# A lead of four tiles instead of three in a graph-and-attention block, with three steps put in another order

## The reference

```python
xn = layernorm(x)
agg = segment_sum(xn[src], dst); ah = agg / max(degree, 1)
lin = xn @ W1.T + b1 + ah @ W2.T + b2
q, k, v = relu(xn @ Wq.T), relu(xn @ Wk.T), xn @ Wv.T        # 16 heads of 32
att = (q @ (k.T v)) / (q @ sum(k) + eps);  x2 = x + lin + att @ Wp.T + bp
xn2 = layernorm(x2)
pooled = sum(xn2 * softmax(xn2 @ attn_w));  gates = softmax(pooled @ gate_w + gate_b)
out = x2 + sum over the best 2 of 8 experts: g_e * gelu(gelu(xn2 @ w1_e + b1_e) @ w2_e + b2_e)
```

## Time and profile before

| | us |
|---|---|
| Runs shown (3): median | 1580.96 |
| Runs shown: lowest, highest | 1580.53, 1581.2 |
| The profiled execution | 1580.07 |
| Its span | 1578.3 |

### The profile page before, as it was taken

One profiled execution on the slowest core, in us unless ns is written; L12 is line 12 of the kernel. 1 busy time (PEld: TensorE's weight loads), 2 busy tenths in 40 slices (PEclk: granted clock), 3 DMA queues, 4 the chain that ended last, 5 costly groups with the idle time before them and its releaser, 6 DMA issues.

```text
span 1578.3 us, 29172 instructions
## 1 busy us (share of the span) xinstructions
PE 1519.8 (96%) x7597; PEld 733.7 (46%) x7598; DVE 1003.1 (64%) x2154; ACT 604.5 (38%) x997; POOL 799.0 (51%) x847
## 2 busy tenths in 40 slices
PE   5999999989999999999999999999999989999997
PEld 2444444444544444444444444444544444444443
DVE  7576522246666667666677666666666666666777
ACT  5777721111333333332333333333333335555554
POOL 4122143646777767777767777767777710000000
PEclk8999999999999999999999999999999989999998
DMA  9977776957777767777767777767777723322323
GB/s 237 262 170 190 189 179 132 217 151 208 234 235 234 234 209 231 234 234 237 233 206 239 239 240 233 234 209 236 236 233 233 233 80 120 107 90 96 106 87 112
DMA packets 166610, 308.64 MB, mean 196 GB/s; under 512 B 71986, under 2 KB 74572, under 8 KB 166260
## 3 DMA queue, kind: packets, MB, share of 16 engines
q0 software_dynamic: 62720, 205.57, 44.3%
q1 hardware_dynamic: 36112, 58.90, 11.7%
q10 hardware_dynamic: 67684, 42.96, 10.7%
HBM read 255.02 MB, written 39.49 MB: 187 GB/s over the span
## 4 chain that ended last, share of the span: by engine, by line
PE 70%; POOL 14%; issue 6%; DVE 3%; DMA 1%; ACT 0%; DVEq 0%; SPq 0%; ACTq 0%
POOL ring L522 14%; PE bank L549 13%; PE bank L554 13%; PE bank L550 12%; PE bank L622 8%; PE bank L623 8%; PE bank L708 2%; PE bank L709 2%; PE bank L710 2%; PE bank L742 2%; PE bank L747 2%; PE bank L743 2%; PE bank L793 1%; PE bank L838 1%; PE bank L800 1%
## 5 line engine op out<-in xcount | busy, mean ns | idle before, releaser
L522 POOL DMA_INDIRECT ring<-table,src_col x784 | 753.5, 961 | 328.9 <-issue 254.5
L622 PE MATMUL bank<-ring,onehot 128*128 x830 | 316.1, 381 | 14.8 <-issue 6.2
L623 PE MATMUL bank<-ring,onehot 128*128 x830 | 315.5, 380 | 0.0
L1238 DVE TENSOR_TENSOR onehot<-bank,dst_col 128x512 f32 x244 | 168.8, 692 | 96.5 <-issue 61.1
L961 ACT ACTIVATE work<-bank,rd 128x512 f32<-128x512 f32 x49 | 33.7, 687 | 336.4 <-DVE rd L1271 336.3
L549 PE MATMUL bank<-wts,xT 128*128 128x512 f16 x392 | 149.1, 380 | 4.1 <-DVE wts L1313 4.1
L550 PE MATMUL bank<-wts,xT 128*128 128x512 f16 x392 | 149.0, 380 | 0.0
L549 PE MATMUL bank<-wts,work 128*128 128x512 f16 x392 | 148.2, 378 | 0.2 <-DVE work L1441 0.2
L550 PE MATMUL bank<-wts,work 128*128 128x512 f16 x392 | 148.3, 378 | 0.0
L622 PEld LDWEIGHTS bank<-ring,onehot 128*128 x830 | 80.9, 97 | 126.5 <-issue 45.6
L623 PEld LDWEIGHTS bank<-ring,onehot 128*128 x830 | 81.1, 98 | 84.8 <-issue 0.9
(11 more groups left out here) (284 smaller groups left out, 2732.5 us busy)
## 6 DMA issues: line engine op xcount, KB each, us to landing
ring<-table,src_col POOLq DMA_INDIRECT x784, 3.7
x_rows<-work ACTq DMA_DIRECT2D x49, 256.0 KB, 3.7
work<-in_x ACTq DMA_DIRECT2D x48, 256.0 KB, 4.3
ring<-x_rows SPq DMA_DIRECT2D x12, 1024.0 KB, 5.3
out_x<-ring SPq DMA_DIRECT2D x12, 1024.0 KB
table<-xT SPq DMA_DIRECT2D x45, 256.0 KB, 3.5
ring<-in_x SPq DMA_DIRECT2D x42, 256.0 KB, 3.7
xT<-in_L_mix_qkv_weight SPq DMA_DIRECT2D x2, 1024.0 KB, 10.1
```

Source lines behind the costliest of these rows:

```text
L522: pool.indirect_dma_start(ring[:, n, :], None, table[:, :], bass.IndirectOffsetOnAxis(ap=ap, axis=0)).then_inc(slot_loaded[n], 16)
L622: mm(ps_agg[:, :], w[:, k, :], rows[:, k, 0:D], start=start, stop=False, skip_group_check=True)
L623: r = mm(ps_agg[:, :], w[:, k, :], rows[:, k, D:2 * D], start=False, stop=stop, skip_group_check=True)
L1238: V.tensor_tensor(onehot[:, bass.ds((q + t) % OG * U, U), :], ps_iota[:, None, :].to_broadcast([P, U, P]), dst_col[:, bass.ds(q % GROUPS * ...
```

## The change

The lead becomes four tiles: `SKEW = 4`, `SLOTS = 5`, a fourth early tile (iteration 36 begins tile 0), and a table of layers in runs of 13, 10, 10, 10 and 1 aggregating layers with plain ones at 14, 25, 36 and 47. The loops now have five bodies and start where the run starts. A fifth ah buffer lies in scratch 11; the last four tiles' rows change places for it (tile 45 in scratch 10, tile 46 in `ksb`), and two waits for their stores follow. Between the phases VectorE takes the next tile's first one-hot and tile `SKEW`'s degrees ahead of M's scale, and ScalarE copies that tile's sum ahead of M's high halves. In VectorE's layer the low half of the turned x2 comes behind the statistics. Behind the choice, the wait for the experts' bias and its largest value come behind the first expert's low half.

```diff
-SKEW = 3
+SKEW = 4
-SLOTS = 4
-EARLY = {39: 0, 42: 1, 45: 2}
-LAYERS = ((1, 4, 3), (4, 12, 3), (12, 13, None), (13, 24, 2), (24, 25, None), (25, 36, 1), (36, 37, None), (37, T, 0),
-          (T, T + 3, None))
+SLOTS = 5
+EARLY = {36: 0, 39: 1, 42: 2, 45: 3}
+LAYERS = ((1, 4, 4), (4, 14, 4), (14, 15, None), (15, 25, 3), (25, 26, None), (26, 36, 2), (36, 37, None), (37, 47, 1),
+          (47, 48, None), (48, T, 0), (T, T + 3, None))
@@ def layers(eng, body):
     for lo, hi, skew in LAYERS:
-        a, b = -(-lo // SLOTS), hi // SLOTS
-        if lo < 4 or b <= a:
-            a = b = hi // SLOTS + 1
-        for i in range(lo, min(a * SLOTS, hi)):
+        n = (hi - lo) // SLOTS
+        if n > 1:
+            with eng.Fori(0, n) as g:
+                for k in range(SLOTS):
+                    body(g * SLOTS + lo + k, skew, (lo + k) % SLOTS)
+            lo += n * SLOTS
+        for i in range(lo, hi):
             body(i, skew, i % SLOTS)
-        if b > a:
-            with eng.Fori(a, b) as g:
-                for k in range(SLOTS):
-                    body(g * SLOTS + k, skew, k)
-            for i in range(b * SLOTS, hi):
-                body(i, skew, i % SLOTS)
@@ natural(t)
-            return (ksb[:, :], work[:, 10], work[:, 11], awb[:, :])[t - (T - NS)].bitcast(F16)
+            return (work[:, 10], ksb[:, :], work[:, 11], awb[:, :])[t - (T - NS)].bitcast(F16)
@@ ScalarE, first phase
                 if i - 2 in EARLY:
+                    if EARLY[i - 2] == SKEW - 1:
+                        stored(act, T - NS)
                     keep_ah(EARLY[i - 2], EARLY[i - 2])
@@ ScalarE, M
             act.wait_ge(s["vt_made"], 1)
+            keep_ah(SKEW, SKEW)
             act.wait_ge(s["scales_made"], 4)
             for j in range(C):
                 F(wm[:, 0, j, :], m_bank[j][:, :], ACT.Copy, scale=kscale[:, j:j + 1]).then_inc(s["mhi_made"], 1)
-            keep_ah(SKEW, SKEW)
@@ VectorE, M
-            stored(dve, T - NS)
+            stored(dve, T - NS + 1)
...
             weigh(0)
+            match_first(SKEW + 1)
+            degrees(SKEW)
             dve.wait_ge(s["spread"], 3)
             spread_max(M_, M_ + 1, bank[3][:, 0:P])
...
             dve.sem_inc(s["scales_made"], 1)
-            match_first(SKEW + 1)
-            degrees(SKEW)
@@ VectorE, layer
-                t = i - 3
-                if real(t):
-                    after(dve, s["x2T_hi"], t + 1)
-                    V.tensor_tensor(tile(t)[:, C:2 * C, :], ps_tx[:, :].rearrange("p (c n) -> p c n", c=C),
-                                    tile(t)[:, 0:C, :], ALU.subtract).then_inc(s["x2T_lo"], 1)
                 t = i - 2
...
                     V.bn_aggr(mv, st6[:]).then_inc(s["mv2_made"], 1)
+                t = i - 3
+                if real(t):
+                    after(dve, s["x2T_hi"], t + 1)
+                    V.tensor_tensor(tile(t)[:, C:2 * C, :], ps_tx[:, :].rearrange("p (c n) -> p c n", c=C),
+                                    tile(t)[:, 0:C, :], ALU.subtract).then_inc(s["x2T_lo"], 1)
@@ VectorE, experts
-            dve.wait_ge(s["b1_loaded"], 32)
-            link(V.tensor_reduce(amax[:, HB_:HB_ + 1], b1t[:], AX.XY, ALU.max, apply_absolute_value=True))
             dve.wait_ge(s["spread"], 5)
             spread_max(W1_, W1_ + 1, bank[2][:, 0:P])
...
             low_part(0, W1_)
+            dve.wait_ge(s["b1_loaded"], 32)
+            link(V.tensor_reduce(amax[:, HB_:HB_ + 1], b1t[:], AX.XY, ALU.max, apply_absolute_value=True))
             on_diagonal(diag_end, (V1_, HB_))
```

More of the change, by code:

```diff
@@ L195, in program @@
         ah = work[:, 7:7 + SLOTS]
-        x_end = ah[:, (T - SLOTS) % SLOTS]
+        x_end = ah[:, (T - 4) % SLOTS]
         ahT, pT = (v.bitcast(F16).rearrange("p (a c n) -> p a c n", a=2, c=C) for v in (ahT_, pT_))
@@ L1074, in layer @@
                     if isinstance(t, int) and t == T - 2:
-                        act.wait_ge(s["turned_ah"], T - SLOTS + 1)
+                        act.wait_ge(s["turned_ah"], T - 3)
                         for a, b in parts(TAIL):
```

## The result

The changed kernel takes 1588.82 us (median of five runs, 1587.18 to 1592.55); beside it the kernel before takes 1581.2 us (five runs, 1580.53 to 1583.27). The ratio is 1.0051, with a 95% interval of 1.0036 to 1.0066: 8 us slower, where 3.9 us faster was forecast.

The account below looks back on a forecast made before the run. TensorE and GpSimd bind the layers in turn. Gains of 2.0 (lead), 0.6 (statistics) and 1.3 us (bias), with 0 for M, sum to 3.9 less: 1577.1 us median, range 1573.0 to 1580.5.

Parts of the forecast that it names:

- the loops of five bodies add no instruction; there are four jumps back before and after: Loops over layers: a remark within the fourth early tile's sum, giving the longer loops no cost.
- its slower case: First phase: DMA engines fill up, turned tiles land late, +7.8 us to 1584.9; chance 0.07.
- The lead by itself: Fourth early tile: 7.7 us paid ahead of the layers, 9.7 gained in them, 2.0 us less in sum.
- the lead is worth nothing: Rival: tile costs 8.0 early, clock falls again, stretch begins at +1; only 1.8 us left, 1579.2; chance 0.22.
- the two small parts: Statistics (0.6 us, lower bound 0.3) and the bias's largest (1.3 us, lower bound 0.8), both after most layers.
- M's order: Layer 1: first wait 1.6 us shorter, a second of some 4.5 opens; stretch start taken as 0, range -3.2 to +1.
- the upper end: Layer 1 on TensorE: +2.6 us at most, if the clock is low again when the second group runs.
- The head start: Rival in layer 1: one-hots come sooner, GpSimd goes through, everything behind comes 3.2 us earlier, 1573.9; chance 0.18.
- Statistics and bias: Next-to-last layers' chain 0.6 us less, first expert's weights 1.3 us less net.

Follow-up runs that it names:

- e1: The changed kernel with VectorE's layers written out, no jump back over layers there: 1579.35 us, ratio 0.9986.
- e12: The changed kernel with VectorE's layers written out and the degrees and aggregate copy back behind M's scale and halves as before: 1576.39 us, ratio 0.9966.
- e5: The changed kernel with the layers written out on TensorE, ScalarE and VectorE: 1583.69 us, ratio 1.0009.
- e7: The kernel before (lead of three) with all three moves (degrees, statistics, bias) and VectorE's layers written out: 1580.65 us, ratio 0.998.
- e11: The kernel before with only the statistics and the bias moved: 1575.91 us, ratio 0.9959.
- e2: The kernel before with the three moves alone (degrees ahead of M's scale, statistics, bias), lead of three: 1577.57 us, ratio 0.9976.
- e10: The kernel before with one move alone, degrees and next tile's one-hot ahead of M's scale: 1582.41 us, ratio 1.0006.
- e6: The kernel before, lead of three kept, with five ah copies and loops of five bodies: 1582.01 us, ratio 1.0004.
- e8: The changed kernel with 228 do-nothing increments on VectorE ahead of its layers: 1584.78 us, ratio 1.0012.
- e9: The changed kernel with do-nothing VectorE increments, 58 ahead of the layers and 32 in each of plain layers 14, 25, 36: 1588.16 us, ratio 1.0037.

## Why the prediction was wrong

**The step that failed** is a half sentence: "the loops of five bodies add no instruction; there are four jumps back before and after". The count was right. What it left out is that a jump has a price that depends on the length and place of its loop. The change made each of VectorE's loops a quarter longer (about 258 to 323 instructions), and two of the four jumps went from 0.6 us to 6.5 and 3.6. TensorE then waited 6.33 and 3.50 us and ran 13 matmuls after each at the lower clock, 2 x 2.8 us: 15.4 us in all, of which 5 came back from GpSimd's pace. The first plain layer came 7.3 us late against e1, the next cycle 3.6. The sum of the prediction has no term for this and no rival either: its slower case was a DMA queue that fills up in the first phase, and no wait for turned tiles appeared there. I set the cost at nothing without asking the trace of before for a jump, though it would have shown four of about 0.6 us, in a place where VectorE's next step otherwise follows at once. That isn't 6.5 us, but it names a resource, the code, for which bounds were due.

The page "Runtime: NRT & Kernel Launch" of the Trainium skill, in its section on instruction fetch mechanics, says: "A taken branch whose target isn't in the current 2-page window forces a DMA fetch of the target page before execution can continue". The instruction packets within the stalls agree with it. The section's size, 256 instructions a block and two blocks held, does not fit the jumps measured here: wherever the ends of such blocks are put, at least one of the sixteen comes out wrong (at best the 3.6 us at 1195 alone), and the packets of q14 are of 8 KB, some 130 instructions by the estimate above. Blocks of 128 fit, with the free number named above; the measurement decides. Weighed beforehand, it would have been a rival on the slower side, whose size no row of before could give.

**The lead by itself** was mis-sized. Forecast: 7.7 us paid ahead of the layers, 9.7 gained in them, -2.0 in sum. Without stalls and added instructions (e1, e12, e5) S is at 357.5 us on average, against 351.2 in the six kernels with a lead of three and four bodies: 6.3 paid. The layers take 921.7 against 927.9: 6.2 gained. The sum is 0, and by the ratios (e1 with e7, e12 with e11) a loss of 1 us that their intervals don't show. The cost was 1.4 us less than forecast and the gain 3.5 less. Of the gain, the first plain layer came at 264.67 us (264.3 forecast) and the last layers at 29.9 (29.84), but the cycles took 208 to 209.8 us where 207.9 was forecast, 626.6 in three where 623.7 was. The 228.1 from which it was worked out lies 0.4 below the mean of the twelve like cycles of those six kernels (228.5), which is part of the miss. So the rival "the lead is worth nothing", given 0.22, came true in its size for this part, and by luck: of the things it was built on, the tile cost 6.3 us ahead of the layers and not 8.0, the first plain layer came near its forecast time, the two small parts gained more than their lower bounds, and the loss lay in the cycles, which it didn't name.

**M's order** behaved as worked out in its mechanism: two waits (2.71 and 3.95 us; 3.5 and 4.5 forecast), layer 1 at 28.84 us where 26.06 + 2.6 = 28.7 was the upper end, and 27.7 and 27.8 in e2 and e10, the lower clock behind the second wait, and the first plain layer at 223.35 (e2) and 224.36 (e10) against 223.96, which is the 0 that was taken. The head start that a rival counted on did not show. Of the clock, the granted clock shows this: before, it was 0.50 for some 3.2 us of layer 1, behind the one wait; in e2 and e10 twice for that long, behind each of the two waits; in the changed kernel once, behind the second wait, for 6.7 us. The windows are those of before, of e10 (two) and of the changed kernel (window and length, busy us and count, granted clock, DMA share, GB/s):

```profile
358.30:361.50 3.20, 3.14 (x8) 0.50 0.41 132
...
357.00:360.30 3.30, 3.30 (x12) 0.50 0.76 204
363.90:367.10 3.20, 3.19 (x8) 0.50 0.80 253
...
369.50:376.20 6.70, 5.47 (x14) 0.50 0.45 153
```

The section on oscillation in the page "TensorE: Matmul & The Clock Gate" of the Trainium skill, by which the prediction has two waits pay the half rate twice, agrees with e2 and e10. It agrees with the changed kernel in the sum, though not in the number of falls. But in e6 and e12, with one wait of 5.1 us as before, the granted clock was 0.50 for 6.6 us too, so these rows don't settle what the new order costs in clock. The time took no upper end from it: in e2 and e10 the first plain layer came within 0.6 us of the kernel before.

**Statistics and bias** went the right way, and further. The waits moved by about what was said, or less: the last tile's from 3.84 to 3.49 (0.6 forecast with the layer before), the first expert's from 3.12 to 1.61 (1.47 forecast), the second low half's stayed at 0.43. Forecast: -1.9 us. Measured: e11 -6.5 us by its ratio (-4.4 to -8.5), -3.9 between the two profiled spans, -3.3 between their tails. About 2 us of it are the terms of the sum. The rest I can't place: the tails of kernels that don't differ there run from 296.3 to 300.6 us (e1 and e8), so a part of what e11 shows may be that spread.

**The slower side** had 0.07 and the range ended at 1580.5. With a term for the code, unknown upwards, neither would have stood. The chance of slower was set on a queue of transfers in the first phase: between 200 and 358 us TensorE's waits show none for turned tiles, and the longest is 1.2 us.

## What to carry to other kernels

A hardware loop's body length and place are part of its cost: when a change makes a looped body longer or shifts it, look at the step behind every jump back on each engine (an idle time put down to "issue") and not only at the instruction count, and write the loop out on the engine whose lateness the critical engine feels. A wait gained or lost at an engine is worth only what the pacing engine lets through; here a stall of VectorE's of 3.6 us went with a cycle 3.6 us longer in one place (layer 20) and one of 3.7 with none in another (layer 42 of e8). Test bundled edits apart: two small moves were worth more alone (0.41%) than the whole bundle even with its fault mended (0.14%), though a part of the 0.41% may be the spread of the tails.

## What was not expected of the hardware

- A jump back of VectorE costs 0.53 to 0.62 us in the good case and 3.5 to 3.9 or 6.5 to 6.7 us in the bad one, with one or two instruction packets in it, beside DMA engines that are busy for 74% of the layers. Shifting the same loop by 228 instructions moves the stall to other jumps (e8), and by 58 and 32 more at a time removes it (e9).
- A semaphore increment issued by VectorE takes 0.11 us (32 in 3.5 us, three times). The plain layers have no room for 3.5 us on VectorE: 1.5 to 1.6 us of them reach TensorE.
- After waits of 2.55 (e6), 2.65 (e2), 3.50, 3.95 and 6.33 us TensorE's next matmuls showed the lower level (0.60 to 0.61 us). After 2.71 us in the changed kernel they showed 0.38 and stayed there; after 3.34 us in e8 they began at 0.39 and fell to 0.63 from 0.7 us on. The length of the wait alone doesn't tell.
